# Stacking query and key levels inside SBUF in an attention kernel, with a reordered lead-in

## The reference, cut to what matters

```
qh = (layernorm(x) @ Wq.T)        # 8 batches, 256 tokens, 32 heads of 16
kh, vh = ctx @ Wk.T, ctx @ Wv.T   # 8 groups of 16, each shared by 4 heads
attn = softmax(qh @ kh.T / 4)     # float32
x = x + (attn @ vh) @ Wfc.T + bfc
x = x + experts(layernorm(x))     # router, 32 experts, top 4; small experts beside them
```

## Time and profile before

| | us |
|---|---|
| median of 3 runs | 1139.05 |
| range of the runs | 1137.99 to 1144.78 |
| the profiled execution's own time | 1136.86 |
| its span in the profile | 1135.1 |
| first real scores (L556) start | 68.2 |
| experts and routing | from some 440 to the end |

### The profile page before, as it was taken

The page is one execution under the profiler, slowest core; times in us unless marked ns, Lnnn a source line. Parts: engine busy times, 40 slices in busy tenths (PEclk is TensorE's granted clock), DMA queues, the critical chain, the costliest instruction groups (busy, mean ns, idle before and its releaser), DMA issues.

```text
span 1135.1 us, 18843 instructions
## 1 busy us (share of the span) xinstructions
PE 1026.3 (90%) x5498; PEld 660.9 (58%) x5500; DVE 423.1 (37%) x1019; ACT 347.1 (31%) x630; POOL 292.9 (26%) x381
## 2 busy tenths in 40 slices
PE   5589999999999988427999999999999999999995
PEld 4356666666655536315666666666666666666662
DVE  5457667666667624691111111111111111111110
ACT  1135544555545533141222222222222222222221
POOL 1211101101000000202344334334334343433442
PEclk9779999999999998757999999999999999999998
DMA  8531451422513003931755776675665767667433
GB/s 307 136 72 48 79 122 39 90 75 52 125 36 71 3 1 133 366 115 42 222 148 141 217 220 146 213 224 144 190 171 150 207 181 199 198 153 221 76 65 48
DMA packets 44120, 154.51 MB, mean 136 GB/s; under 512 B 9136, under 2 KB 12336, under 8 KB 38960
## 3 DMA queue, kind: packets, MB, share of 16 engines
q1 hardware_dynamic: 26448, 111.23, 31.0%
q0 software_dynamic: 17632, 42.74, 19.2%
HBM read 116.46 MB, written 37.22 MB: 135 GB/s over the span
## 4 chain that ended last, share of the span: by engine, by line
PE 53%; issue 1%; DMA 0%; ACT 0%; DVEq 0%; POOL 0%; DVE 0%; POOLq 0%; ACTq 0%
PE y_ps L1324 18%; PE g_ps L1307 15%; PE u_ps L1307 15%; PE xt_ps L1300 3%; PE at_ps L1316 2%; DMA xg<-xd,gidx 0%; POOL out_x L1211 0%; DVEq L1288 0%; ACT sg L1236 0%; ACT yb L1243 0%; ACT xT L1232 0%; DVE aT L1265 0%; DVEq L1289 0%; DVE a L1278 0%; DVE a L1279 0%
## 5 line engine op out<-in xcount | busy, mean ns | idle before, releaser
L1324 PE MATMUL y_ps<-W,aT 128*128 x468 | 215.5, 597 | 2.5 <-DVE aT L1265 2.5
L1211 POOL DMA_INDIRECT out_x<-yb,yidx x78 | 125.3, 1606 | 298.0 <-DMA out_x<-yb,yidx 134.7
L309 ACT ACTIVATE pt<-stp 128x512 f32<-128x512 f32 x256 | 139.0, 596 | 173.2 <-PE stp L556 172.2
L411 DVE TENSOR_REDUCE mx<-s 128x2 f32<-128x512 f32 x256 | 164.0, 682 | 69.4 <-PE s L542 68.0
L1307 PE MATMUL g_ps<-W,xT 128*128 x624 | 183.3, 437 | 0.9 <-ACT xT L1232 0.9
L1307 PE MATMUL u_ps<-W,xT 128*128 x624 | 181.3, 433 | 0.0
L1307 PEld LDWEIGHTS u_ps<-W,xT 128*128 128x128 f32 x624 | 119.1, 191 | 49.9 <-issue 0.8
L1307 PEld LDWEIGHTS g_ps<-W,xT 128*128 128x128 f32 x624 | 113.5, 192 | 39.0 <-issue 2.4
L1278 DVE TENSOR_TENSOR a<-u_ps,sg 128x192 f32<-128x192 f32 x78 | 27.9, 358 | 287.6 <-ACT sg L1236 287.6
L1324 PEld LDWEIGHTS y_ps<-W,aT 128*128 128x128 f32 x468 | 83.5, 192 | 78.3 <-issue 78.3
L1236 ACT ACTIVATE sg<-g_ps 128x320 f32<-128x320 f32 x78 | 34.1, 437 | 305.5 <-PE u_ps L1307 305.5
(11 more groups left out here) (155 smaller groups left out, 932.2 us busy)
## 6 DMA issues: line engine op xcount, KB each, us to landing
W<-in_wts SPq DMA_DIRECT2D x32, 2048.0 KB, 8.4
qd<-q SPq DMA_DIRECT2D x8, 768.0 KB, 3.6
qst<-qd SPq DMA_DIRECT2D x8, 768.0 KB, 7.5
ctxT<-in_ctx SPq DMA_DIRECT2D x8, 512.0 KB, 11.6
qst<-qd SPq DMA_DIRECT2D x8, 512.0 KB, 10.1
xd<-r_xn SPq DMA_DIRECT2D x16, 256.0 KB, 2.0
out_x<-xs SPq DMA_DIRECT2D x1, 4096.0 KB, 13.9
xs<-in_x SPq DMA_DIRECT2D x2, 1536.0 KB, 13.6
```

What stands on the lines that cost most here:

```text
L309: act.activation(pt[g % 2][:, 2 * (j % 2) + r, :, :], stp[n % STP][:, :, :], ACT.Exp, scale=DH ** -0.5).then_inc(exp_done, 1)
L411: dve.tensor_reduce(mx[j // CH % 2][:, 2 * h:2 * h + 2], s1[r][:, :, :], AX.X, ALU.max)\
L1211: pool.indirect_dma_start(out[:, :], bass.IndirectOffsetOnAxis(yidx[p][:, :], 0), yb[p][:, :], None, compute_op=ALU.add).then_inc(y_added, ...
L1324: m = pe.matmul(y_ps[:, :], aT[p][:, c, :], W[:, bass.ds(buf, 1), GW + c * D:GW + (c + 1) * D].rearrange("p a d -> p (a d)"), start=(c == ...
```

## The change

- Levels go from SBUF to SBUF without DRAM: each level of K and of Q is copied by one DMA per block of 16 rows of the stack (`ROWS_OF_Q`, `ROWS_OF_K`), six for K (64 KB each) and six for Q (256 KB each), as soon as that level is ready. `q3` and the context get two buffers.
- Heads are taken in chunk order: round j of chunk c takes heads c, 4 + c, 8 + c and so on (`head`), one of each group, so that a quarter of Q's columns is one chunk.
- Batch 0's Q is projected in four chunks into four PSUM banks of their own (`q0_ps`: the three banks of the scores and that of the values), each split and stacked by itself (`stack_q0`, six DMAs of 64 KB each); its transpositions use the two banks of the maxima.
- LEAD is 8: a chunk's maxima are transposed and split in rounds 0, 4, 8 and 12, and are needed four rounds later. `stack_max` has four DMAs of 2 KB instead of two of 4 KB. In SyncE's order of batch b the first of them stands behind the K and Q copies of batch b + 1 and the context.
- Statistics are taken per batch, for batches 3 to 7 in the rounds; the root is ScalarE's Ln and Exp, and VectorE corrects it with three small operations (`refine`) instead of a reciprocal.
- Constants for `vx` and `kst` are written by GpSimd instead of VectorE.
- In the lead-in, batch 1's transpositions, Q and K stand between the steps of the maxima. Wv, Wfc, Bfc and the later groups of x are loaded later.
- Most side work stands one round later than before (`transpose_x` and `project_v` in rounds 1 and 2 instead of 0 and 1, and so on).

```diff
-RUNS = ((0, 3), (1, 2), (2, 1))
-ROWS_QK = DH * sum(n for _, n in RUNS)
+ROWS_QK = 6 * DH
 ROWS_ST = ROWS_QK + 2
-LEAD = 9
+ROWS_OF_Q = ((0, 16, 32), (48, 64), (80,))
+ROWS_OF_K = ((0, 48, 80), (16, 64), (32,))
+X_BEGINS = (0, 2, 4, 10)
+LEAD = 8
 CH = 4
 NC = J // CH
...
-        ctxT = sb("ctxT", [P, C, S], F32)
+        ctxT = [sb(f"ctxT{i}", [P, C, S], F32) for i in range(2)]
...
         xnT = sb("xnT", [P, C, S], F32)
-        q3 = sb("q3", [P, 3, C * S], BF16)
+        q3 = [sb(f"q3{i}", [P, 3, C * S], BF16) for i in range(2)]
         k3 = [sb(f"k3{i}", [P, 3, S], BF16) for i in range(2)]
...
+        def head(j, r):
+            return (2 * (j % CH) + r) * C + j // CH
...
             load_x(0)
             load_ctx(0)
-            sp.dma_start(Wk[:, :, :], wk).then_inc(kvw_loaded, DMA)
-            sp.dma_start(Wv[:, :, :], wv).then_inc(kvw_loaded, DMA)
+            sp.dma_start(Wk[:, :, :], wk).then_inc(wk_loaded, DMA)
             sp.dma_start(Wq[:, :, :], wq).then_inc(wq_loaded, DMA)
-            for k in range(1, len(GROUPS)):
-                load_x(k)
+            sp.dma_start(Wv[:, :, :], wv).then_inc(wv_loaded, DMA)
+            load_x(1)
+            load_ctx(1)
+            def stack_k(b):
+                if b >= 2:
+                    sp.wait_ge(st_ready, (b - 1) * H)
+                for n, ready in ((0, k_hi), (1, k_mid), (2, k_lo)):
+                    sp.wait_ge(ready, b + 1)
+                    for at in ROWS_OF_K[n]:
+                        dst = kst[b % 2][at:at + DH, :, :].rearrange("p g t -> p (g t)")
+                        sp.dma_start(dst, k3[b % 2][:, n, :]).then_inc(k_stacked, DMA)
+            def stack_q0(c):
+                for n, ready in ((0, q0_hi), (1, q0_mid), (2, q0_lo)):
+                    sp.wait_ge(ready, c + 1)
+                    for at in ROWS_OF_Q[n]:
+                        dst = qst[0][at:at + DH, c::C, :]
+                        sp.dma_start(dst, q0_parts(c)[n]).then_inc(q0_stacked[c], DMA)
+            def stack_q(b):
+                if b >= 2:
+                    sp.wait_ge(st_ready, (b - 1) * H)
+                for n, ready in ((0, q_hi), (1, q_mid), (2, q_lo)):
+                    sp.wait_ge(ready, q_counts(b, 1) + 1)
+                    for at in ROWS_OF_Q[n]:
+                        dst = qst[b % 2][at:at + DH, :, :].rearrange("p h t -> p (h t)")
+                        sp.dma_start(dst, q3[b % 2][:, n, :]).then_inc(q_stacked, DMA)
+            def next_ctx(b):
+                if b < NB:
+                    sp.wait_ge(v_full, b - 1)
+                    load_ctx(b)
+            def stack_max(n):
+                b, c = n // NC, n % NC
+                sp.wait_ge(mt_empty, n + 1)
+                for l in range(2):
+                    for t in range(TT):
+                        dst = qst[b % 2][ROWS_QK + l:ROWS_QK + l + 1, c::C, t * P:(t + 1) * P]
+                        sp.dma_start(dst, nm[n % 2][t * G:(t + 1) * G, l, :]).then_inc(m_ready[n % 2], DMA)
+            stack_k(0)
+            stack_q0(0)
+            load_x(2)
+            for c in range(1, C):
+                stack_q0(c)
             sp.dma_start(Wfc[:, :, :], wfc).then_inc(w_loaded, DMA)
             sp.dma_start(Bfc[:, :], bfc).then_inc(w_loaded, DMA)
-            def store_q(b):
...
-                stack_max(n)
             for b in range(NB):
                 if 0 < b < NB - 1:
                     stack_k(b + 1)
                     stack_q(b + 1)
                 next_ctx(b + 2)
-                for j in range(3, J, CH):
+                for j in range(0, J, CH):
                     if chunk_at(b, j) < NB * NC:
                         stack_max(chunk_at(b, j))
-                    if j == 11 and b < NB - 2:
-                        store_q(b + 2)
-                        store_k(b + 2)
         @block.gpsimd
...
-            def deviations(k):
-                t0, t1 = GROUPS[k]
-                act.wait_ge(var_ready, k + 1)
-                act.activation(std[:, t0:t1], mv[:, t0:t1, 1], ACT.Sqrt, bias=eps[:, :]).then_inc(std_ready, 1)
+            def deviations(b):
+                ts = slice(b * TT, b * TT + TT)
+                act.wait_ge(var_ready, b + 1)
+                act.activation(lnv[:, ts], mv[:, ts, 1], ACT.Ln, bias=eps[:, :]).then_inc(ln_ready, 1)
+                act.wait_ge(ln_ready, b + 1)
+                act.activation(root[:, ts], lnv[:, ts], ACT.Exp, scale=-0.5).then_inc(root_ready, 1)
...
             k_first(0)
+            x0_evac(0)
+            x0_evac(1)
+            for c in range(C):
+                q0_first(c)
             v_evac(0)
             deviations(1)
-            x_evac(0, 0)
-            x_evac(0, 1)
-            q_first(0, 0)
-            q_first(0, 1)
-            deviations(2)
-            deviations(3)
             k_first(1)
...
             for b in range(NB):
                 for j in range(J):
                     exponentials(b, j)
-                    if j == 0 and b < NB - 2:
-                        x_evac(b + 2, 0)
...
+                m = dve.memset(mx[i][:, :], 0.0)
+            m.then_inc(mx_clear, 1)
+            def moments(b):
+                if b * TT in X_BEGINS:
+                    dve.wait_ge(x_loaded[X_BEGINS.index(b * TT)], DMA)
+                for t in range(b * TT, b * TT + TT):
                     dve.bn_stats(st6[:, t, :], xs[:, t, :]).then_inc(stats, 1)
-                for t in range(*GROUPS[k]):
+                for t in range(b * TT, b * TT + TT):
                     dve.wait_ge(stats, t + 1)
                     m = dve.bn_aggr(mv[:, t, :], st6[:, t, :])
                 m.then_inc(var_ready, 1)
-            def invert(k):
-                t0, t1 = GROUPS[k]
-                dve.wait_ge(std_ready, k + 1)
-                dve.reciprocal(rstd[:, t0:t1], std[:, t0:t1]).then_inc(rstd_ready, 1)
-                dve.wait_ge(rstd_ready, k + 1)
+            def refine(b):
+                ts = slice(b * TT, b * TT + TT)
+                dve.wait_ge(root_ready, b + 1)
+                dve.scalar_tensor_tensor(fix[:, 0, ts], mv[:, ts, 1], EPS, root[:, ts], ALU.add,
+                                         ALU.mult).then_inc(fixed, 1)
+                dve.wait_ge(fixed, 2 * b + 1)
+                dve.scalar_tensor_tensor(fix[:, 1, ts], fix[:, 0, ts], -0.5, root[:, ts], ALU.mult,
+                                         ALU.mult).then_inc(fixed, 1)
+                dve.wait_ge(fixed, 2 * b + 2)
+                dve.scalar_tensor_tensor(rstd[:, ts], fix[:, 1, ts], 1.5, root[:, ts], ALU.add,
+                                         ALU.mult).then_inc(rstd_ready, 1)
+                dve.wait_ge(rstd_ready, b + 1)
             def normalise(b, t):
...
+                if j == 4:
+                    split_max(0)
+                    q_split(1, 0)
+                if j == 5:
+                    moments(2)
+                if j == 7:
+                    q_split(1, 1)
+                row_max(0, j)
+            refine(2)
             normalise(2, 0)
             normalise(2, 1)
-            for j in range(LEAD):
-                if j and j % CH == 0:
-                    split_max(j // CH - 1)
-                row_max(0, j)
             for b in range(NB):
                 for j in range(J):
                     if j == 0 and b >= 2:
                         add_out(b - 2, 1)
-                    if j == 2 and b:
+                    if j % CH == 0 and chunk_at(b, j) < NB * NC:
+                        split_max(chunk_at(b, j))
+                    if j == 3 and b:
                         weigh(b - 1, 3)
-                    if j == 5 and b < NB - 2:
+                    if j == 4 and b < NB - 3:
+                        moments(b + 3)
+                    if j == 6 and b < NB - 2:
                         q_split(b + 2, 0)
-                    if j in (6, 10, 14):
+                    if j in (7, 11, 15):
                         weigh(b, j // 4 - 1)
-                    if j in (7, 8) and b < NB - 3:
-                        normalise(b + 3, j - 7)
-                    if j == 9 and b:
+                    if j == 8 and b < NB - 3:
+                        refine(b + 3)
+                    if j in (8, 9) and b < NB - 3:
+                        normalise(b + 3, j - 8)
+                    if j == 10 and b:
                         add_out(b - 1, 0)
-                    if j == 12 and b < NB - 2:
+                    if j == 13 and b < NB - 2:
                         q_split(b + 2, 1)
-                    if j == 13 and b < NB - 2:
+                    if j == 14 and b < NB - 2:
                         k_split(b + 2)
-                    if j % CH == CH - 1 and chunk_at(b, j) < NB * NC:
-                        split_max(chunk_at(b, j))
                     b1, j1 = maxima_of(b, j)
...
+            def project_q0(k):
+                for c in range(C):
+                    m = pe.matmul(q0_ps[k], Wq[:, c, k * P:(k + 1) * P], xnT[:, c, :], start=(c == 0), stop=(c == C - 1))
```

(89 more changed lines are left out.)

284 lines of the change are left out of this document (135 added, 149 removed).

## The result

The kernel after takes 1204.08 us (median of 4 runs, 1203.13 to 1206.86), beside 1138.52 before (4 runs): ratio 1.0574, interval 1.0524 to 1.0624. The profiled execution took 1203.5 us with a span of 1201.7, 66.6 more than before. The prediction said slower, at 1153; the time is 32 us above the end of its range.

What follows compares the result with a forecast made beforehand. TensorE, busy 90% of the span, was taken as the bound, with time to win only where it idles or is clocked low. 1136.9 - 20 - 5 + 3 + 35 + 2 = 1151.9, about 1153 us as median; range 1112 to 1172.

Steps and rivals of the forecast that it cites:

- The lead-in: Before the first real scores: fewer TensorE gaps and an earlier start of steady rounds, 20 us gained.
- The moments and roots: Statistics on VectorE and ScalarE inside the rounds of five batches: +3 us in all, range 0 to 6.
- the new wait: TensorE's scores at round 4 wait for maxima queued behind the copies: 5.7 us in five batches, 6.7 in batch 1, 35 us.
- copies at the rate of the loads: Rival: SBUF to SBUF copies as fast as loads, so nothing waits; about 1117 us, chance 0.28.
- the landing: When round 4's maxima arrive: 17.2 us from first K issue to landing before, adjusted for six Q copies to 17.8 us.
- the release: The last scores of a batch, which free the stacking; landing and need times are counted from here.
- The term of the copies: Six Q copies of 256 KB at 1.9 us each instead of 1.8, added to the 17.2 us queue time.
- the nearest row: Profile reading for one copy: third Q DMA, 256 KB onto 16 partitions, landing 2.0 us after the second.
- The slow end: Upper bound for the copies, 2.5 us each: maxima land at 21.4 us, stalls 57 us in all.
- The need: When round 4 needs its maxima: 12.1 us after the release, 11.1 in batch 1.
- stall and clock: Rival: each stall also lowers TensorE's clock, 2.5 us more in six batches, 15 us; 1168 us, chance 0.06.
- the side work: Moved one round later, so V no longer waits for the output's addition in round 0: -5 us, range 0 to -6.

Runs made afterwards that it cites:

- run 5: Changed kernel's lead-in, heads, copies and statistics, with lead 9, the kernel before's order of rounds, and the chunk needed next queued ahead of the copies: 1121.24 us.
- run 8: The kernel of run 5 with the spread rows of run 7 added: 1116.20 us, ratio 0.9800.
- run 6: Separate kernel with copies only, no computation, timing 256 KB DMAs: 2.14 us each from SBUF to 16 neighbouring rows, 1.2 us to rows 8 apart.
- run 9: Changed kernel with seven extra matmuls, results unread, ahead of the scores of round 4 in batches 1 to 6: 1191.09 us.
- run 2: Changed kernel with the maxima's transposition moved behind the round's values and their split behind VectorE's reductions, queue unchanged: 1194.54 us.
- run 1: Changed kernel with SyncE issuing each batch's first chunk of maxima ahead of the K and Q copies: 1168.97 us.
- run 3: Changed kernel with queue order K copies, maxima of round 0, Q copies, maxima of round 4, context, plus the late transposition of run 2: 1141.74 us.
- run 10: Changed kernel, lead 8 kept, with the edits of run 3 and run 7 together: 1136.40 us.
- run 7: Changed kernel with each block's 16 rows, for K and Q, on every sixth partition of 96 instead of 16 neighbours: 1162.19 us.

## Why the prediction was wrong

**Right.** The lead-in: 22.9 us won where 20 was said, with the first scores at 45.3 ("near 45"); some 3 of them go again in batch 0 (runs 5 and 8). The moments and roots: nothing (run 5), said +3. The mechanism and place of the new wait: the scores of round 4 of batches 1 to 6 on the small DMAs behind the copies. And that few written partitions, not the source in DRAM, set the rate of a copy (run 6); the rival "copies at the rate of the loads" (0.28, 1117 us) has no ground left. What spoke for it said nothing: at 2.0 us for 256 KB, 64 KB of K take some 0.5, and were issued 0.47 apart, so they could not pile up.

**Wrong, the landing.** Step "17.2 + 6 x (1.9 - 1.8) = 17.8 us after the release", which gave stalls of 5.7 and 6.7. Measured in batch 1: from the release at 95.1 the scores had to wait until 116.84, 21.7 us, 3.9 more. The term of the copies was mis-sized: from Q's first issue (99.04) to the last landing (115.06) were 16.0 us, where the row before had 12.6 and the prediction added 0.6, so 2.8 of the 3.9 lie there. A copy takes 2.14 us (run 6) and mostly 2.2 in the kernel, not 1.9; the nearest row had been read right, as 2.0, and then averaged down to 1.8 over all six thirds. K's issuing made 1.0: six of 0.60 us instead of 0.43 put Q's first issue 3.9 us behind the release instead of 2.9. And 17.2 was a median read as an end: the view of the pair behind the bulk in the kernel before,
```profile
DMA to landing us min/median/max: 6.9/7.5/8.1
```
says that the second, issued at 120.31, landed at 128.4, not "near 127.5". These 0.9 us came back by luck, because the maxima now land 1.8 us behind Q's last copy instead of 2.6. The slow end, 21.4 us, came so near by luck too: its 2.5 us a copy is too much by 0.3, and the longer issuing of K is not in it. With 49.6 us in six stalls and 2.6 in batch 0 the term is 52 instead of 37.

**The need, right but for a wait.** It was 12.1 us after the release in batch 1 (said 11.1), 13.4 in batches 2 to 5 and 11.7 in batch 6 (said 12.1). L647's wait in round 0 (1.2 us in batch 1, 0.8 in the others), explained below, lies within each of them; it hid that much of the late landing. So 22% on the landing of batch 1, less 1.0 us on the need, became 45% on its stall (9.7 for 6.7). That a batch takes "some 42 us" before was a misreading as well, without effect on the sum: 109 to 151 is not a whole batch, and batches 1 to 5 take 44.9 to 46.3.

**Wrong, the clock.** "TensorE idle for 7 us ... fell ... about 5.2 us after the idling began" was read rightly: in batch 1 it fell 5 us after, in the others after 2.0 to 4.0. The forecast's own stalls, 5.7 and 6.7 us, passed even the 5.2, so the rival "stall and clock" belonged into the forecast instead of standing beside it at 0.06. Its size, 15 us, agrees with the 15.5 of run 9's estimate.

**Missing, the transposition inside the rounds.** The prediction priced the lead of 8 only in the queue. With it the last two reductions of a chunk fall into an odd round, which has no values behind its maxima's matmuls, and the transposition is the first side work of the next: in batch 1 of the kernel before, the values, the next scores and two matmuls of Q lay between (115.97 to 118.82), now only the scores. This is L647's 20.3 us of waits, 23 times some 0.9. Put behind the values, the transposition waits no more, at a gain of 9.5 us (run 2). The row for it stood in the profile: two reductions of 683 ns per round on an engine whose answer is now needed at once.

**Wrong sign, the side work.** "V waits for the addition of the output in round 0 ...; by round 1 it has been done: -5". V's wait is gone, but Q's projection (L580) now waits for the same additions, 6.6 us, and the output projection (L667) for Q's split, 4.4: 11.0 instead of 7.3 with V's and Q's, +3.7. The transpositions of values no longer wait for ScalarE, 2.6 less, so the whole is +1.1. A wait for a late producer was taken to vanish when its consumer moves, without asking which matmul takes the place.

The stretch from the first to the last scores is 92.4 us longer. TensorE waits 75.0 of them: 52.2 + 20.3 + 1.1, 2.8 for a transposition of x in batch 0, and 1.4 less in small ones. It is busy 17.2 longer, 15.5 by the clock as estimated above; 1.7 stay open. With 22.9 less ahead of it and 2.8 less behind it that is the 66.6 in the trace. The terms are not independent, as runs 1 to 3 show: a wait that goes lets the next come forward. By the runs that undo parts: lead, rounds and queue back, -82.8 (run 5); rows spread on top, -5.0 (run 8). With lead 8 kept: queue order and late transposition -62.3 (run 3), rows spread on top -5.3 (run 10), and 20.2 left that only run 8, with the lead of 9 and its order of side work, gives back; no run parts these two.

## To carry to other kernels

Before the depth of a pipeline is cut by a step, list everything that the last step of slack covered, in each queue and in each engine's order of instructions: here it hid 20 us of a DMA queue and the time of two reductions, and cutting it, with the orders that it brought, cost 83 us (run 5 beside the kernel after), in a kernel whose other edits were worth 17. A small transfer that an engine needs soon must be issued ahead of the bulk, or the bulk must be made short; where a copy writes few partitions, choose their addresses spread out, which is free if the contraction's order is. And where a predicted wait is the difference of two long times, give the range from their errors, not from its own size.

## What the runs showed of the hardware that was not expected

- Writing 256 KB onto 16 neighbouring partitions takes 2.14 us, onto 16 partitions 6 or 8 apart 1.2 us (run 6), from the same source with the same issue; in the kernel this alone gave 42 us (run 7).
- Issuing 256 KB from SyncE takes 0.42 us for 16 rows out of DRAM and 0.60 us for 128 partitions as the source (run 6); in the kernel one of each batch's twelve copies took 1.2 to 1.6.
- A stall costs more than its length: the granted clock fell to 1.2 GHz 2.0 to 5.0 us into the stalls of 7.6 to 9.7 us and was low for 2.8 to 5.5 us of the work behind them; the round took 3.9 to 6.0 us instead of 3.4. Seven matmuls without use, 6.2 us, in each stall kept it at 2.4 GHz in batches 2 to 5, where 1.7 to 2.2 us of idling was left; in batch 1 (3.9 left) they did not, and in batch 6 (2.0 left) it fell all the same (run 9).
